# Second attention's first two score blocks issued inside the last mixed batch, with two preparation steps moved between engines and batches

## What is computed

```
x = x + tanh(g_xattn[0]) * attention_0(layernorm(x), ctx)      # 32 query heads, capped logits
h = layernorm(x)
x = x + tanh(g_ffn[0]) * (h @ W_base.T + b_base                # "base" product
        + sum_e alpha_e * (h @ A_e.T) @ B_e.T)                 # low-rank experts, alpha = softmax(prior + routing logits)
qp = patches(layernorm(x))                                     # 4 patches of 128 columns
q, k = Wq qp + bq, Wk qp + bk;  val = Wv patches(ctx) + bv     # 8 heads of 8
scores = where(mask, q.k / sqrt(8), -1e9)
o = gelu(softmax(scores) val)
x = x + tanh(g_xattn[1]) * (Wo o + bo) * masks
x = x + tanh(g_ffn[1]) * mean of the two best experts' relu    # routed feed-forward
```

## Time and profile before

| | |
|---|---|
| median of 3 runs | 953.14 us (952.55 to 953.42) |
| profiled execution, its own time | 953.01 us |
| its span, first to last instruction | 951.2 us |
| PE, DVE, ACT, POOL busy | 885.7, 616.2, 324.5, 415.8 us |
| mean granted TensorE clock | 0.955 |

### The profile page before, as it was taken

How to read it: one execution, slowest core, us unless ns; L and a number is a source line. 1 busy time by engine, 2 the same in 40 slices (tenths; PEclk the granted TensorE clock), 3 DMA queues, 4 the chain that set the end, 5 groups by cost and what they waited for, 6 DMA issues and landing times.

```text
span 951.2 us, 13808 instructions
## 1 busy us (share of the span) xinstructions
PE 885.7 (93%) x4739; PEld 721.5 (76%) x4739; DVE 616.2 (65%) x1061; ACT 324.5 (34%) x581; POOL 415.8 (44%) x423
## 2 busy tenths in 40 slices
PE   5999999999999999999999999998999999667993
PEld 4778878977878887877887877766799995655772
DVE  6975674376575366576446577677898865876345
ACT  5333133224133214214214214231566773612230
POOL 4651442153352153153243162337888616537551
PEclk9999999999999999999999999999899995569997
DMA  9020120020120011111002002031255306323448
GB/s 315 14 89 1 34 89 1 12 82 8 34 89 1 14 45 45 34 45 45 12 11 79 1 1 79 1 113 39 65 170 154 89 5 228 133 67 115 140 143 310
DMA packets 42242, 70.13 MB, mean 74 GB/s; under 512 B 7034, under 2 KB 14779, under 8 KB 42051
## 3 DMA queue, kind: packets, MB, share of 16 engines
q1 hardware_dynamic: 37060, 56.97, 18.5%
q0 software_dynamic: 3680, 12.06, 3.9%
q10 hardware_dynamic: 1440, 0.24, 0.1%
HBM read 52.61 MB, written 10.22 MB: 66 GB/s over the span
## 4 chain that ended last, share of the span: by engine, by line
PE 80%; DVE 9%; DMA 3%; issue 3%; ACT 1%; POOL 1%; SPq 1%; ACTq 0%; DVEq 0%
PE ps L1373 17%; PE ps L1375 16%; PE ps L1374 16%; PE ps L1494 6%; PE ps L1486 6%; PE ps L1623 6%; PE ps L1611 3%; PE ps L1502 3%; DMA rows_in<-h_rows,gather_i 2%; PE ps L1604 2%; PE ps L1672 1%; DMA rb<-in_router_b 1%; DVE h L922 1%; DVE stats L916 1%; PE ps L1718 1%
## 5 line engine op out<-in xcount | busy, mean ns | idle before, releaser
L528 POOL TENSOR_TENSOR q_t<-rot_a,rot_b 128x512 f32<-128x512 f32 x64 | 82.6, 1291 | 152.7 <-DVE rot_b L967 152.7
L965 DVE TENSOR_TENSOR rot_a<-ps,cos 128x512 f32<-128x512 f32 x80 | 55.2, 689 | 87.3 <-PE ps L1375 86.7
L1373 PE MATMUL ps<-xt_hi,wq_hi 128*128 128x512 f32 x256 | 107.6, 420 | 0.5 <-DVE rot_b L967 0.5
L1373 PE MATMUL ps<-wo_hi,at_hi 128*128 128x512 f32 x256 | 106.7, 417 | 0.4 <-DVE at_lo L1073 0.4
L1375 PE MATMUL ps<-xt_hi,wq_lo 128*128 128x512 f32 x256 | 101.1, 395 | 0.0
L1374 PE MATMUL ps<-xt_lo,wq_hi 128*128 128x512 f32 x256 | 101.0, 394 | 0.0
L1375 PE MATMUL ps<-wo_hi,at_lo 128*128 128x512 f32 x256 | 100.2, 391 | 0.0
L1374 PE MATMUL ps<-wo_lo,at_hi 128*128 128x512 f32 x256 | 99.8, 390 | 0.0
L760 ACT ACTIVATE ps<-ps 128x512 f32<-128x512 f32 x64 | 37.2, 582 | 178.6 <-PE ps L1486 178.6
L773 ACT ACTIVATE at_hi<-ps 128x512 fp32r<-128x512 f32 x64 | 38.2, 597 | 171.5 <-PE ps L1502 171.5
L1078 DVE TENSOR_TENSOR X<-ps,X 128x512 f32<-128x512 f32 x64 | 44.2, 690 | 73.9 <-PE ps L1375 73.6
(11 more groups left out here) (218 smaller groups left out, 2125.7 us busy)
## 6 DMA issues: line engine op xcount, KB each, us to landing
wq_raw<-in_wq SPq DMA_DIRECT2D x8, 1024.0 KB, 5.4
wo_raw<-in_wo SPq DMA_DIRECT2D x8, 1024.0 KB, 5.1
w_raw<-in_we SPq DMA_DIRECT2D x8, 1024.0 KB, 5.7
X<-in_x SPq DMA_DIRECT2D x4, 512.0 KB, 13.1
wk_raw<-in_wk SPq DMA_DIRECT2D x8, 256.0 KB, 2.9
q_t<-in_ctx_t SPq DMA_DIRECT2D x2, 1024.0 KB, 9.9
wv_raw<-in_wv SPq DMA_DIRECT2D x4, 512.0 KB, 3.8
ctx_s<-in_ctx SPq DMA_DIRECT2D x8, 256.0 KB, 4.7
```

What stands on the lines that cost most here:

```text
L528: nc.gpsimd.tensor_tensor(dst, rot_a[:, r % 2, :], rot_b[:, r % 2, :], ALU.add).then_inc(rope_ok, 1)
L965: nc.vector.tensor_tensor(heads(rot_a[:, r % 2, :]), heads(bank), bcast(cos[:, :], 4), ALU.mult)
L1373: nc.tensor.matmul(dst, w_hi, x_hi, start=start and k == 0, stop=False)
```

## The change

Four things move. (1) PE issues `context(0, 0)` and `scores(0, 0, 0)` inside the last mixed batch, between its base product and `lora_out(6)`; `scores(0, 0, 1)` goes between `lora(7)` and `lora_out(7)`, behind a wait for `zw_ok`, because its bank still holds batch 7's routing product until `z_w` has been read. (2) DVE does `row_max(0, 0)` and `less_max(0, 0)` inside its last mixed batch, between the maximum of the logits and the wait for `lg_e`. (3) The ones in `q3`'s penalty row are written by an ACT activation after `zeros(0)`, where a DVE memset after batch 3 wrote them. (4) DVE scales the output weights (`wo1g`) at b == 5 instead of b == 3. `s_max` and `s_sub` get a place of their own behind `alpha`, since they are now live beside the mixed stage's tiles.

```diff
@@ arena
         alpha = sb("alpha", [P, 2, ET])
-        assert place[0] <= at_2
+        s_max = sb("s_max", [P, 2, 4])
+        s_sub = sb("s_sub", [P, 2, D])
+        assert place[0] <= at_1 + 24 * KT * D + 7680
...
         place[0] = at_1 + 16 * KT * D
-        s_max = sb("s_max", [P, 2, 4])
-        s_sub = sb("s_sub", [P, 2, D])
@@ ACT
                 mix(b, b % 2, b < B - 1)
                 zeros(b)
+                if b == 0:
+                    nc.scalar.activation(q3[PARTS:PARTS + 1, :, :, :].rearrange("p j g n -> p (j g n)").rearrange("p (a c) -> p a c", c=P),
+                                         bcast(ones[PARTS:PARTS + 1, :], 16), ACT.Copy).then_inc(pen_ok, 1)
@@ DVE, mix
                 if not last and not first:
                     mix_lo(b + 1, 1 - j)
+                if last:
+                    row_max(0, 0)
+                    less_max(0, 0)
                 ve.wait_ge(lge_ok, CREDIT + b + 1)
@@ DVE, batch of the second attention
                 for u in range(H1):
-                    row_max(b, u)
-                    less_max(b, u)
+                    if not first or u > 0:
+                        row_max(b, u)
+                        less_max(b, u)
@@ DVE, mixed batches
                 if b == 3:
-                    nc.vector.tensor_scalar(wo1g[:, :], wo1[:, :], tanh_g[0:E1 + 1, 1:2], None, ALU.mult).then_inc(wo1_ok, 1)
-                    nc.vector.memset(q3[PARTS:PARTS + 1, :, :, :].bitcast(F32), 1.0).then_inc(pen_ok, 1)
                     ve.wait_ge(pen_raw, 16)
...
                 if b == B - 3:
                     evict(1, 1, 7)
+                    nc.vector.tensor_scalar(wo1g[:, :], wo1[:, :], tanh_g[0:E1 + 1, 1:2], None, ALU.mult).then_inc(wo1_ok, 1)
@@ PE
                 based(b, j)
+                if last:
+                    context(0, 0)
+                    scores(0, 0, 0)
                 lora_out(b - 1, 1 - j)
...
             lora(B - 1, 1)
+            pe.wait_ge(zw_ok, CREDIT + B)
+            scores(0, 0, 1)
             lora_out(B - 1, 1)
...
-            context(0, 0)
-            scores(0, 0, 0)
-            scores(0, 0, 1)
             batch(0, 0, first=True)
```

More of the change, by code:

```diff
@@ L1025, in mixed, with row_max, less_max @@
                 nc.vector.scalar_tensor_tensor(t_b[:, j, :], ps[:, 4 + j, :], tanh_g[:, 2:3], bbg[:, :], ALU.mult, ALU.add).then_inc(tb_ok, 1)
+            def row_max(b, u):
+                ve.wait_ge(s2_mm, CREDIT + 8 * b + u + 1)
+                nc.vector.tensor_reduce(s_max[:, u % 2, :], heads(ps[:, 2 + u % 2, :]), AX.X, ALU.max).then_inc(mx_ok, 1)
+            def less_max(b, u):
+                ve.wait_ge(mx_ok, CREDIT + 8 * b + u + 1)
+                ve.wait_ge(p_ok, CREDIT + 8 * b + u - 1)
+                nc.vector.tensor_tensor(heads(s_sub[:, u % 2, :]), heads(ps[:, 2 + u % 2, :]),
+                                        s_max[:, u % 2, :].unsqueeze(2).to_broadcast([P, 4, P]), ALU.subtract).then_inc(sb_ok, 1)
             def mix(b, j, first=False, last=False):
@@ L1139, in values @@
                                         ALU.add).then_inc(cv_ok, 1)
[L1141 to L1149, removed]
             def over_sums(b, j):
@@ L1567, in lora_out @@
                 nc.tensor.matmul(ps[:, 4 + j, :], z_wt[:, j, :], lb[:, :], start=False, stop=True).then_inc(y_mm, 1)
[L1569 to L1587, removed]
             def context(b, j):
@@ L1605, in scores, with mix, proj @@
                                  k_blk[0:PARTS + 1, j, u % 2, u // 2, :, :], start=True, stop=True).then_inc(s2_mm, 1)
+            def mix(b, j, last=False):
+                if not last:
+                    turn_rows(1, b + 1, 1 - j, 1 - j)
+                routed(b, j)
+                lora(b - 1, 1 - j)
+                based(b, j)
+                if last:
+                    context(0, 0)
+                    scores(0, 0, 0)
+                lora_out(b - 1, 1 - j)
+            def proj(b, j, rows, bank):
+                pe.wait_ge(hc_ok, CREDIT + b + 1)
+                nc.tensor.matmul(ps[:, bank, :], wqk1[:, :], rows[:, j, :], start=True, stop=True).then_inc(qk_mm, 1)
+            for b in range(1, B):
+                mix(b, b % 2, last=b == B - 1)
+                if B - 4 <= b < B - 2:
+                    pe.wait_ge(qk_ev, CREDIT + b - B + 4)
+                    proj(b - B + 4, b % 2, p_w, 7)
+            lora(B - 1, 1)
+            pe.wait_ge(zw_ok, CREDIT + B)
+            scores(0, 0, 1)
+            lora_out(B - 1, 1)
             def turn(b, u):
```

## The result

The changed kernel took 955.18 us at the median of 15 runs (951.65 to 958.68), the kernel before beside it 952.32 (950.24 to 954.7). The ratio is 1.0027, with a 95% interval of 1.0016 to 1.0038: slower, by 2.9 us at the medians. The forecast was 953.5 us, 0.5 over before, so the time lies in the stated range (0.1 us inside its upper end) and on the stated side, but beyond the likeliest case. It was one of the rivals that happened.

What follows compares the result with a forecast made beforehand. A four-engine loop, not PE, was taken to bound the mixed batches. PE gains 2.71 - 1.8 = 0.9 us, eaten in the last batch, then +0.5: 953.0 + 0.5 = 953.5 us, range 951.3 to 955.3.

Steps and rivals of the forecast that it cites:

- the likeliest case: Whole kernel: a time of 952.6 to 954.2 us, given a chance of 0.55.
- own sign of being wrong: Mixed stage: a granted clock below 1.00 near 625 was named as one sign that the forecast is wrong.
- The clock rival: PE's wait before batch 3's turn of rows grows to 2.15 us and the clock falls: 955.1 us, chance 0.12.
- DVE's block: After mixed batch 3: taking wo1g and the memset from DVE gives PE 2.7 us, low end 2.5.
- ACT's row: Behind zeros(0), ahead of ht_hi(2): a 1.91 us ACTIVATE, less 0.1 overlap, delays the four-engine loop by 1.8 us.
- Moving wo1g: DVE at b == 5, before batch 6's routing logits: costed at nothing, 0.7 us if the cover were gone.
- DVE's new wait: Last mixed batch: lg_n(7) held to 662.3 for the score block, z_w(7) 1.7 us later, second s_sub +0.5.
- the case of +0.9: End of mixed stage: h held until POOL's qk_lo ends, making the second s_sub 0.9 us later.
- The sum: PE 0.9 us early up to the last batch, eaten there, then +0.5 at the fourth score block's release: 953.5 us.
- the clock recovers later: Head of second attention: clock stays low 3 us longer, PE loses 1.5: 955.0 us, chance 0.10.

Runs made afterwards that it cites:

- the hole filled: Eight unused TensorE products added in the hole behind ACT's row, against the preparation alone (0.9993, 951.53 us) and against the changed kernel (0.9994, 952.07 us).
- the covered row: ACT's ones row moved from ahead of ht_hi(2) to behind lg_e(1), against the changed kernel and without early scores; 0.9988 with early scores, 0.9963 without.
- early scores alone: Kernel before plus the early context and score blocks only, ones row and wo1g left on DVE after batch 3; 1.0007, 953.01 us.
- preparation with the row covered: Kernel before with ACT's ones row behind lg_e(1) and wo1g at b == 5, no early scores; 0.9963, 949.38 us.
- preparation alone: Kernel before with ACT's ones row behind zeros(0) and wo1g at b == 5, no early scores; 1.0007, 953.03 us.
- the second profile: The changed kernel itself measured and profiled again, nothing altered, against the kernel before; 1.0012, 953.94 us.
- the changed one with the row covered: Changed kernel with ACT's ones row moved from ahead of ht_hi(2) to behind lg_e(1), early scores kept; 0.9988, 951.31 us.

## Why the prediction came out as it did

The sign and the range held; the forecast's likeliest case did not, and that the range held was in part luck. It was built on 953.0 us for the kernel before, whose median beside the changed one was 952.32: the same 2.9 us on top of 953.14, the median on record, would have been 956.0, above the range. The prediction's own sign of being wrong, a granted clock below 1.00 near 625, was there, and the turn after the first projection came 2.2 us late instead of 0.9 early. Step by step:

**The clock rival happened.** The step that failed is the weight of 0.12 for "the clock falls in the new hole", and with it the sum's silence on the clock up to the last batch. The hole was 2.41 us, the clock fell in every profile with it, and it cost 2.60 us by turn 6 (29.38 against 26.78), where I had priced the loop's part alone at 1.6. That part cost less: from the turn to the z transpose 2.92 us (626.04 to 628.96) instead of 1.79 (623.32 to 625.11), 1.1 more. But the base product behind it ran at half speed too and outlasted the loop: PE's next turn follows `lora_out` without a wait (634.75), 8.71 us after the one before it instead of 6.04. The evidence was in the earlier trace rows, a wait of 2.14 us and a fall behind it. I discounted it for being one case, and that was wrong.

**DVE's block.** 2.7 forecast, 2.5 as low end, 2.5 measured, in each kernel without the block (from the turn before it to turn 6, 26.78 - 20.17 = 6.61 with the hole filled against 27.21 - 18.09 = 9.12 before). So it was the low end, though not for the 0.48 us of idle time: the mask tile's operation begins beside POOL's add and takes 0.9 us.

**ACT's row.** 1.91 us long as worked out. In the loop it costs 2.07, not 1.8: I took off 0.1 for an overlap with the fills, and there is none; `ht_hi` lost the overlap that it had with them besides. From the start of the fills to that of `ht_hi` are 3.12 us (620.21 to 623.33), before 1.06. That there was no slack was right, and the covered row shows it: turn 3 at 6.00 again.

**Moving wo1g.** Nothing forecast; 0.28 us (655.53) of DVE time in front of a wait for `ht_hi`. Right as argued, not tried alone.

**DVE's new wait.** Forecast: `lg_n(7)` held by 3.4 us, `z_w(7)` 2.6 later than without it (1.7 and the shift of 0.9), the second `s_sub` 1.4 later (0.5 and 0.9). Measured in the early scores alone: 3.41, 2.48 and 1.62. The mechanism was right, and the sizes as far as two profiles can tell. `h` ran 1.38 us beside `qk_lo`, as in the case of +0.9. By the Trainium skill ("SBUF — State Buffer", "Who interferes with whom"), a `tensor_scalar` can take a two-port mode, and whichever of VectorE and GpSimd issues first then holds the shared ports for its whole instruction while the other waits. The traces agree, in both orders: begun behind POOL's instruction, `h` ends 0.27 to 0.29 us after it (the kernel before, early scores alone, preparation with the row covered); begun 0.11 before POOL's add in the changed kernel, `h` takes 0.54 and the add 1.55 instead of 1.27. The covered preparation without early scores has the same collision (1.28), and of the two profiles of the changed kernel one has it (1.51) and one hasn't (0.54): a tenth of a microsecond decides, and it isn't a price of the early scores alone.

**The sum.** At turn 6 the parts add up: -2.5 for the block, 2.1 for the row and 2.6 for the fall are 2.2, and the changed kernel is 2.18 late. At `z_w(7)` they no longer do: 2.48 for the scores and 1.20 for the preparation are 3.68, against 4.66 and 4.70. In the preparation alone `lg_n(7)` is only 1.44 late, because before ACT waited 0.69 us for the stack's DMAs ahead of `lg_e(7)`, and that wait took up part of the delay; PE's score block, for which DVE waits with early scores, has no such reserve, and `lg_n(7)` is held by all of it (48.15 against 45.92 in the scores alone). That the parts fit at the second `s_sub` (1.62 + 2.22 = 3.84, against 3.90 in the first profile) is chance: both parts have the collision of `h`, the first profile of the changed kernel hasn't, and the second profile, which has, is at 5.05. At the last `o_inv` 0.68 and 1.35 stand against 3.42 and 4.21: there the kernel before had 6.4 us of low clock behind the second `s_sub`, both parts 3.4, the changed kernel 5.5 and 3.4, and each part's time is 0.9 us too low by it. So the long slow stretch of the changed kernel (10.4 us) is not what the rival "the clock recovers later" priced: most of it lay where PE waited, and behind the second `s_sub` there was less of it than before. What sets its length is open.

**What I would have had to forecast:** 953.0 - 2.5 + 2.1 + 2.6 and 0.7 to 1.6 for the scores, 955.9 to 956.8, against 956.67 and 956.92 in the two profiled executions. The measured differences of the medians, 2.9 and 1.65 us, are at the low end of this sum and below it. The profiled execution was the third slowest of fifteen and the slowest of twelve (that of the preparation alone, with the same fall, was among the faster ones of its kernel). So whether the fall comes in every execution isn't known: the profiles show it in three of three.

## What to carry to other kernels

Before work is put on an idle engine, look at where in its queue it goes: ACT was idle for four of six microseconds per batch, but the row was put into the other two, which lie in the loop. A wait of DVE on another engine's product belongs behind everything whose result that engine needs next; the same pair of instructions made `z_w(7)` 3.4 us late ahead of `lg_n` (44.70 against 41.28) and not at all behind `z_w` (41.23). And price a new hole in TensorE's work by the clock as well as by its length, if the trace has one fall behind a hole of that length.

## What the runs showed of the hardware

A hole of 2.41 us in otherwise dense TensorE work was followed by 6.8 us at 1.2 GHz in three profiles of three; eight products of no use in the hole kept 2.4 GHz in two of two. Holes of 0.35 to 1.43 us in the mixed batches before the last brought no fall in any. But the length of one hole doesn't decide alone. At the end of the stage PE waits 1.71 us for `z_w(7)` in two kernels, the changed one with the row covered and the early scores alone:

```profile
660.60 0.33 PE L1569 MATMUL ps<-ident,z_w 128*128 128x128 f32 x1 [1.71 <-DVE z_w L1060]
```

```profile
663.00 0.33 PE L1567 MATMUL ps<-ident,z_w 128*128 128x128 f32 x1 [1.71 <-DVE z_w L1057]
```

In the first the clock fell 1.3 us later, at 661.9, in the second only at 669.7, behind a further wait of 3.66 us.

The clock came down for about 3.4, 6.8 or 10.2 to 10.4 us at the head of the second attention (0.91, 0.83 and 0.74 over 660 to 680), once as two stretches of 3.4 us, and it differed between two executions of one kernel.

A VectorE scaling of 128x512 elements took 0.54 us alone and 1.38 when it began just behind a GpSimd subtraction of 1.26 us; begun 0.11 us before a GpSimd addition it took 0.54, and the addition 1.55 instead of 1.27. A scaling of 8x512 elements took 0.91 us instead of 0.41 beside a GpSimd addition.
